# The middle part of a two-layer convolution kernel rebuilt on a ring of 20 tiles, with the depthwise taps taken off TensorE

## The reference, cut to what matters

```
h = gelu(batchnorm(conv1x1(haar(x), w_c1)))        # 8 x 128 x 128 x 128
o = dwconv3x3(h, dw_w, dw_b)                       # nine taps a channel
o = layernorm_chw(o)                               # one mean and variance an image
o = conv1x1(gelu(conv1x1(o, pw1)), pw2)
h2 = o + h
x = x + haar_inverse(gelu(batchnorm(conv1x1(h2, w_c2))))
```

## Time and profile before

| | us |
|---|---|
| median of 3 runs (lowest to highest) | 5953.61 (5949.91 to 5953.89) |
| the profiled execution, its own time | 5952.43 |
| its span, first to last instruction | 5950.4 |
| busy in the span: PE, DVE, ACT, POOL | 5103.1, 4918.3, 4124.4, 220.3 |
| middle part, first y1 load to first load of the third part | 2934.3 to 4505.9 |

### The profile page before, as it was taken

The page is one execution under the profiler, slowest core; times in us unless marked ns, Lnnn a source line. Parts: engine busy times, 40 slices in busy tenths (PEclk is TensorE's granted clock), DMA queues, the critical chain, the costliest instruction groups (busy, mean ns, idle before and its releaser), DMA issues.

```text
span 5950.4 us, 66856 instructions
## 1 busy us (share of the span) xinstructions
PE 5103.1 (86%) x13460; PEld 2331.3 (39%) x13460; DVE 4918.3 (83%) x5569; ACT 4124.4 (69%) x6080; POOL 220.3 (4%) x267
## 2 busy tenths in 40 slices
PE   1889999999999999999868988889887777777775
PEld 0334444444444444444334544445443222222222
DVE  6998988989898898875388888888856888888887
ACT  4877777777777777665245555556546888888887
POOL 0000000000000000000000000000000111111111
PEclk6999999999999999999989999999999999999998
DMA  8999999999999999887612322223216999999999
GB/s 338 370 360 426 427 426 427 420 427 420 427 418 427 427 418 427 341 334 294 251 62 86 110 85 85 85 85 110 87 65 161 237 235 236 236 235 237 235 237 225
DMA packets 279307, 1627.01 MB, mean 273 GB/s; under 512 B 32816, under 2 KB 33200, under 8 KB 115376
## 3 DMA queue, kind: packets, MB, share of 16 engines
q1 hardware_dynamic: 187056, 1022.13, 43.5%
q0 software_dynamic: 36864, 268.45, 21.7%
q10 hardware_dynamic: 55296, 335.57, 13.5%
HBM read 954.94 MB, written 671.09 MB: 273 GB/s over the span
## 4 chain that ended last, share of the span: by engine, by line
PE 55%; DMA 21%; DVE 11%; issue 7%; ACT 4%; DVEq 0%; ACTq 0%; POOLq 0%; SPq 0%; POOL 0%
DMA out_x<-arena 18%; PE ps L678 13%; PE ps L666 11%; PE ps L661 11%; PE ps L785 6%; PE ps L774 4%; PE ps L753 4%; PE ps L744 4%; DMA arena<-in_x 3%; ACT arena L623 2%; DVE arena L1065 2%; DVE arena L1051 2%; PE ps L762 1%; DVE arena L1079 1%; DVE arena L1195 1%
## 5 line engine op out<-in xcount | busy, mean ns | idle before, releaser
L858 PE MATMUL ps<-arena,c2T 128*128 128x512 f32 x2048 | 1033.2, 657 | 380.9 <-ACT arena L616 369.8
L661 PE MATMUL ps<-arena,w_right 128*128 128x512 f32 x2048 | 974.2, 598 | 42.7 <-DVE w_right L1000 22.8
L666 PE MATMUL ps<-arena,w_center 128*128 128x512 f32 x2048 | 967.2, 595 | 24.4 <-DVE arena L1079 24.4
L678 PE MATMUL ps<-arena,w_c1b 128*128 128x512 f32 x2048 | 964.7, 615 | 7.8 <-DVE small L1029 7.6
L1195 DVE SCALAR_TENSOR_TENSOR arena<-arena,taps (+1 forms) x1280 | 860.0, 745 | 4.0 <-issue 0.2
L410 ACT ACTIVATE arena<-ps,small 128x1024 f32<-128x1024 f32 x512 | 568.1, 1110 | 371.1 <-PE ps L666 371.0
L1051 DVE SCALAR_TENSOR_TENSOR arena<-arena,shift 128x2048 f32<-128x2048 f32 x256 | 601.3, 2349 | 250.8 <-PE ps L666 132.5
L858 PEld LDWEIGHTS ps<-arena,c2T 128*128 128x128 f32 x2048 | 405.7, 207 | 1007.7 <-ACT arena L616 565.8
L616 ACT ACTIVATE arena<-ps,small 128x512 f32<-128x512 f32 x1024 | 713.7, 778 | 105.1 <-DVE arena L1294 94.4
L388 ACT ACTIVATE ps<-arena 128x1024 f32<-128x1024 f32 x512 | 526.3, 1028 | 170.2 <-ACT arena L410 160.3
L661 PEld LDWEIGHTS ps<-arena,w_right 128*128 128x128 f32 x2048 | 385.3, 190 | 552.3 <-issue 470.3
(11 more groups left out here) (161 smaller groups left out, 4839.8 us busy)
## 6 DMA issues: line engine op xcount, KB each, us to landing
arena<-in_x SPq DMA_DIRECT2D x400, 1024.0 KB, 15.6
out_x<-arena ACTq DMA_DIRECT2D x256, 1024.0 KB, 8.9
arena<-out_x SPq DMA_DIRECT2D x256, 1024.0 KB, 16.3
out_x<-arena POOLq DMA_DIRECT2D x256, 1024.0 KB, 17.0
arena<-in_x SPq DMA_DIRECT2D x112, 1152.0 KB, 15.4
y_dram<-arena ACTq DMA_DIRECT2D x128, 512.0 KB, 8.5
arena<-y_dram SPq DMA_DIRECT2D x128, 512.0 KB, 3.5
h_dram<-arena SPq DMA_DIRECT2D x256, 256.0 KB, 2.0
```

The costliest lines, as they stand in the source:

```text
L661: mm(ps[:, r, :], w_right[:, :], u_buf[k][:, 2 * r:2 * r + 2, 2:W + 2], start=False, stop=False, skip_group_check=True)
L666: last = mm(ps[:, r, :], w_center[:, :], v_buf[k][:, r * BANK:(r + 1) * BANK], start=False, stop=True, skip_group_check=True)
L678: last = mm(ps[:, 4 + s % 2, :], w_c1b[:, q, :], cells[:, q // 2, q % 2, :, :], start=(q == 0), stop=(q == 3))
L858: last = mm(ps[:, 4 * k + q, :], c2T[:, q, :], h2_in[s // 2][:, k * HC:(k + 1) * HC], start=True, stop=True)
```

## The change: a ring of tiles in place of two planes

The planes `h_pad` and `o_all` go. `h_rows` holds the h of 20 tiles and a row on either side, `o_ring` the o of 20 tiles. One loop without rounds runs on every engine over steps s = 0 to 148, written out, without loop instructions: step s makes h of tile s, finishes o of tile s - 2, and does the old half of tile q = s - 19. The layernorm of an image is done inside of the steps 2 after its last tile (`norm_step`).

Taps: ACT puts the centre tap of a tile (1024 elements) into two PSUM banks, DVE adds five taps there, one instruction of 1024 each, the next tile's taps between those of this one, and `finish_o` adds the sum that POOL has made of the three others and writes o. POOL runs three TENSOR_SCALAR and two TENSOR_TENSOR of 1024 a tile. PE has no taps. `first_conv` and `second_conv` write the same two banks, one after the other. h2 is written over o in the ring by one instruction and stored by one DMA of 512 KB. The Gram matrix is added up in PSUM over an image. The setup tensors of the other parts lie in the arena at other addresses.

```
+POOL_TAPS = [(1, 0), (1, 2), (0, 0)]
+DVE_TAPS = [(0, 1), (0, 2), (2, 0), (2, 1), (2, 2)]
+EARLY = 3
+RING = 20
+OLD_LAG = RING - 1
+        z_bank = ps[:, 0:2, :]
+        def tap_order(s):
+            late = [(s - 2, i) for i in range(EARLY, len(DVE_TAPS) + 1)]
+            early = [(s - 1, i) for i in range(EARLY)]
+            return [(t, i) for pair in zip(late, early) for t, i in pair if 0 <= t < TILES]
...
 SP
-            planes(0, old=False)
-            with sp.Fori(1, B) as b:
-                planes(b)
-            planes(B, new=False)
+            for s in range(TILES + OLD_LAG):
+                q = s - OLD_LAG
+                if s < TILES:
+                    if s >= 2:
+                        sp.wait_ge(h_ready, nth(s - 2))
+                    sp.dma_start(y1_in[s % 2], y1_dram[s]).then_inc(y1_loaded[s % 2], 16)
+                if q >= 0:
+                    sp.wait_ge(h2_ready, nth(q))
+                    if q >= 4:
+                        sp.wait_ge(h2_stored[q % 4], 16 * (q // 4))
+                    sp.dma_start(h2_dram[q], o_ring[q % RING]).then_inc(h2_stored[q % 4], 16)
...
 POOL
+            for t in range(TILES):
+                n = t * POOL_OPS
+                pool.wait_ge(h_ready, nth(t))
...
+                pool_tap(pool_b, t, POOL_TAPS[1])
...
+                pool_tap(pool_a, t, POOL_TAPS[0])
+                if t:
+                    pool.wait_ge(dw_acc, o_made(t - 1))
+                pool.wait_ge(pool_step, n + 2)
+                pool.tensor_tensor(pool_sum, pool_a, pool_b, ALU.add).then_inc(pool_step, 1)
+                pool.wait_ge(pool_step, n + 3)
+                pool_tap(pool_a, t, POOL_TAPS[2])
+                pool.wait_ge(pool_step, n + 4)
+                pool.tensor_tensor(pool_sum[:, first:last], pool_sum[:, first:last], pool_a[:, first:last],
+                                   ALU.add).then_inc(pool_step, 1)
...
 ACT
+            for s in range(TILES + OLD_LAG + 1):
+                q = s - OLD_LAG
+                if s < TILES:
+                    make_h(s)                 # waits: h2_ready of tile s - 20, y1_loaded of s
+                if 0 <= q < TILES:
+                    make_a(q)                 # 128 x 1024 gelu of z_bank; waits: pw1_done of q
+                if q >= 1:
+                    copy_hT(q - 1, 0)
+                b = norm_step(s)
+                if b is not None:
+                    square_root(b + (2 * B + 2))
+                    warm_gelu(b + 1)
+                if s < TILES:
+                    put_tap(s)                # waits: o of tile s - 2 made
+                if q >= 1:
+                    copy_hT(q - 1, 1)
+                if 0 <= s - 2 < TILES:
+                    square_o(s - 2)
...
 PE
+            for s in range(TILES + OLD_LAG + 2):
...
+                if 0 <= q < TILES:
+                    first_conv(q)             # waits: h2_ready of q - 1
...
+                if 1 <= q <= TILES:
+                    turn_h2(q - 1, 0)
+                if q >= 2 and b is None and after is None:
+                    gram_half(q - 2, 1)
+                if 0 <= q < TILES:
+                    second_conv(q)            # waits: a_ready of q
...
+                if 1 <= q <= TILES:
+                    turn_h2(q - 1, 1)
+                    gram_half(q - 1, 0)
...
 DVE
+            for s in range(TILES + OLD_LAG + 2):
...
+                if b is not None:
+                    o_moments(b)
+                for n, (t, i) in enumerate(tap_order(s)):
+                    if i == len(DVE_TAPS):
+                        finish_o(t)           # waits: POOL's sum of t
+                    else:
+                        add_tap(t, i)
...
+                if 0 <= q < TILES:
+                    make_h2(q)                # waits: pw2_done of q
+                if b is not None:
+                    o_weights(b)
```

More of the change, by code:

```diff
@@ L301, in _ @@
             sp.wait_ge(bn1_ready, 1)
[L303 to L318, removed]
[L320 to L327 removed]
+            for s in range(TILES + OLD_LAG):
[9 more added lines that the diff above has]
+                    sp.dma_start(h2_dram[q], o_ring[q % RING]).then_inc(h2_stored[q % 4], 16)
+            for k in range(4):
+                sp.wait_ge(h2_stored[k], 4 * TILES)
             sp.wait_ge(bn2_ready, 1)
@@ L514, in _ @@
             act.wait_ge(bn1_ready, 1)
[L516 to L574, removed]
+            def make_h(t):
+                p = t % RING
+                if t >= RING:
+                    act.wait_ge(h2_ready, nth(t - RING))
+                act.wait_ge(y1_loaded[t % 2], 16 * (t // 2) + 16)
+                y1 = rows(y1_in[t % 2])
+                if p == 0 and t % NT:
+                    nc.scalar.activation(h_rows[:, RING * TROWS + 1, 1:HW + 1], y1[:, 0, :], ACT.Gelu,
+                                         bias=h_bias, scale=h_scale)
+                if p == RING - 1 and t % NT != NT - 1:
+                    nc.scalar.activation(h_rows[:, 0, 1:HW + 1], y1[:, TROWS - 1, :], ACT.Gelu,
+                                         bias=h_bias, scale=h_scale)
+                nc.scalar.activation(h_tile(t), y1, ACT.Gelu, bias=h_bias, scale=h_scale).then_inc(h_ready, 1)
@@ L766, in gram_tile @@
-            def gram_tile(b, j):
-                n = b * (2 * NT) + j * 2
-                pe.wait_ge(gram_added, nth(b * NT + j, 1))
-                for half in range(2):
-                    pe.wait_ge(hT_ready, nth(n + half))
-                    for c in range(4):
-                        last = mm(ps[:, 0, 0:P + 1], hT_buf[half][:, c, 0:P], hT_buf[half][:, c, :],
-                                  start=(half == 0 and c == 0), stop=(half == 1 and c == 3))
-                last.then_inc(gram_done, 1)
@@ L778, in dw_half @@
-            def dw_half(b, j, half, last_tile=False):
-                below = any(dy == 2 for dy, _ in PE_TAPS) and not last_tile
-                pe.wait_ge(h_ready, nth(b * NT + j, -int(below)))
-                pe.wait_ge(dw_put, nth(b * (2 * NT) + j * 2 + half))
-                for n, (dy, dx) in enumerate(PE_TAPS):
-                    last = mm(ps[:, 6 + half, :], tap_diag[:, n, :],
-                              h_pad[:, bass.ds(j * TROWS + (4 * half + dy), 4), dx:dx + HW],
-                              start=False, stop=(n == len(PE_TAPS) - 1), skip_group_check=True)
-                last.then_inc(dw_done, 1)
@@ L790, in planes_step @@
-            def planes_step(b, j, new, old):
-                early = isinstance(j, int)
-                before = old and not (early and j == 0)
-                if old:
-                    first_conv(b - 1, j, back=1 if early and j == 0 else 2)
-                if before:
-                    turn_h2(b - 1, j - 1)
-                if new and not early:
-                    dw_half(b, j - DW_LAG, 0)
-                if before:
-                    gram_tile(b - 1, j - 1)
-                if new and not early:
-                    dw_half(b, j - DW_LAG, 1)
-                if old:
-                    second_conv(b - 1, j)
@@ L828, in _, with first_conv @@
-            pe.wait_ge(bn1_ready, 1)
-            planes(0, old=False)
-            with pe.Fori(1, B) as b:
-                planes(b)
-            planes(B, new=False)
+            def first_conv(q):
+                if q % NT == 0:
+                    pe.wait_ge(w_ready, q // NT + 1)
+                if q:
+                    pe.wait_ge(h2_ready, nth(q - 1))
+                for half in range(2):
+                    last = mm(z_bank[:, half, :], w_pw1b[:, :], o_ring[q % RING][:, half * BANK:(half + 1) * BANK],
+                              start=True, stop=True)
+                last.then_inc(pw1_done, 1)
@@ new lines, in second_conv, with turn_h2 @@
+            def second_conv(q):
+                pe.wait_ge(a_ready, nth(q))
+                for half in range(2):
+                    last = mm(z_bank[:, half, :], pw2T[:, :], a_buf[:, half * BANK:(half + 1) * BANK],
+                              start=True, stop=True)
+                last.then_inc(pw2_done, 1)
+            def turn_h2(q, half):
+                n = q * 2 + half
+                pe.wait_ge(h2_ready, nth(q))
+                if n:
+                    pe.wait_ge(hT_ready, nth(n - 1))
+                for c in range(4):
+                    at_ = half * BANK + c * P
+                    last = nc.tensor.transpose(ps[:, 2, c * P:(c + 1) * P],
+                                               o_ring[q % RING][:, at_:at_ + P], ident[:, :])
+                last.then_inc(hT_done, 1)
@@ new lines, in gram_half @@
+            def gram_half(q, half):
+                b, m = q // NT, q % NT
+                pe.wait_ge(hT_ready, nth(q * 2 + half))
+                if m == 0 and half == 0 and b:
+                    pe.wait_ge(gram_added, b)
+                for c in range(4):
+                    last = mm(ps_gram, hT_buf[half][:, c, 0:P], hT_buf[half][:, c, :],
```

(41 more changed lines are left out.)

336 lines of the change are left out of this document (164 added, 172 removed).

## The result

| | before | after |
|---|---|---|
| median, us (lowest to highest of 5) | 5953.61 (5949.91 to 5954.72) | 5974.98 (5968.61 to 5987.89) |
| span of the profiled execution | 5950.4 | 5969.1 |
| h2 of tile 0 done | - | 3110.1 |
| first load of the third part | 4505.9 | 4523.8 |

The ratio is 1.004, 95% interval 1.0027 to 1.0053: slower, by 21 us and clear of noise, where 88 us faster was forecast. A second comparison on another chip gave 5978.73 against 5951.77, 1.0045 (1.0028 to 1.0061).

A forecast was written before the change was run, and what follows sets the result against it. Before, DVE was full within rounds and all else waited between; after, a loop through SP. h2 of tile 0 at 3096, then 108 x 10.8 + 9, 19 x 6.9 + 3, third part at 4419: 5866 us, range 5740 to 6045.

The forecast's parts named there:

- The loop through SP's order: Beside an old image, y1's load waits behind h2's store; load, gelus, second_conv and make_h2 close a loop of 10.8 us.
- rival B: DVE sets the pace in the middle, 8.5 us a step, needing y1 landed in 2.0 us: 5618 us; chance 0.08.
- PE's clock, 0.2 us a step: second_conv takes some 1.8 us longer at 1.2 GHz; for one in nine that adds 0.2 us a step.
- the 2.25 for full clock: From the start of second_conv to DVE's make_h2, which now needs both halves: 2.25 us.
- D: TensorE stays at 1.2 GHz in second_conv: 1.8 us more a step, 12.4 in all, 6039 us; chance 0.12.
- A: Main forecast: the loop through SP sets a period of 10.8 us (10.0 to 11.5), 5866 us (5780 to 5942); chance 0.68.
- The load, 4.1: y1's load in the loop beside an old image, put at 4.1 us, bounds 3.2 to 4.9.
- The two gelus, 2.30 with the start: On ACT, gelu of h 1.15, gelu of z 1.10, and 0.05 ahead of them: 2.30 us a step.
- Start and end: h2 of tile 0 at 3096; 19 tiles old alone at 6.9 us plus 3; third part's first load at 4419.
- C: POOL sets the pace at 12.7 us a tile, making the kernel slower: 6147 us; chance 0.12.
- DVE's write to PSUM: DVE's taps adding into PSUM cost 0 to 0.1 us more an instruction; the low end was used.
- Layernorm: 30 us between rounds becomes small DVE instructions within steps: 1.5 us each, nine for six images, 3 for the last.

The follow-up runs named there:

- experiment 3: Changed kernel with y1's load issued before the store: 5941.99 us; that with the store held until the load landed: 5820.28; changed kernel storing 8 of 1024 columns: 5863.98.

## Why the prediction was wrong, by its own steps

- *The mechanism was right.* The loop through SP's order was named before any run and is what the rows show; cutting it at SP or at ACT brings the step to 8.3 and 8.6. Without it the forecast would have been rival B's 5618, and the kernel with the load ahead came to 5668.
- *The step that failed is a size: PE's clock, 0.2 us a step.* I let one `second_conv` in nine fall to 1.2 GHz. It took 1.06 us a step: `second_conv` to `make_h2` is 3.08 on average and 2.02 at full clock. By the 1.8 that 1.2 GHz costs, that is six in ten and not one in nine: 25 of 108 lay wholly at 1.2 GHz, 58 in part. This term is 0.86 x 108 = 93 us over its forecast; at its forecast size the time would have been some 5882, an estimate, and so faster than before. Against the 2.45 in the sum only 0.63 a step shows, 68 us, because the 2.25 for full clock was 0.23 too high. I had the two numbers that spoke for more: PE busy for 6.3 of 10.6 with 3 us of pause, and image 0 at 0.77 with gaps of the same kind. Against D I argued that PE would then be busy all the time; it was busy for 807 of 1170. A and D are not rivals: D is a price within A.
- *The load, 4.1.* 4.36 to the landing and 0.12 to the gelu, where 4.1 and 0.05 were forecast: 36 us in all, some 16 of them by the 13 late loads. The bounds 3.2 to 4.9 held it; the reason given, that it queues behind the store, did not (experiment 3).
- *The two gelus, 2.30 with the start.* 0.2 more on average, 16 to 22 us: in one step of each image z waits for the layernorm, and that step takes 13.7 to 15.6. I had put the layernorm on DVE alone.
- *Start and end.* h2 of tile 0 at 3110 for 3096. 4 of these 14 are the first part's addresses, costed at nothing. The larger part is the layernorm of image 0, which stands in no term of the sum: two distances from `finish_o` to `finish_o` are 13.3 and 14.2 (3076.81 to 3104.32) where POOL's pace gives 8.34, 11 us. POOL gave 3 back. The nineteen tiles of the old half alone took 129.7 for 134. In sum 4523.8 for 4419: 14 at the start, 96 in the steps (1270.6 for 1175), less 4.
- *POOL.* 8.3 us a tile for 8.5: 1.118 for the tap (1.1), 2.36 for the add (2.2). C did not come. The estimate of 2.25 for the add from the Trainium skill, GPSIMD Engine Reference, section 3.1, was 0.1 low. The rule of the Trainium skill, SBUF — State Buffer, section "Who interferes with whom", that a DVE instruction with one input in SBUF doesn't hold off POOL, agrees with the trace: all 128 of POOL's first adds took 2.34 to 2.37 us, though DVE was busy for the whole of some and for a tenth of others.
- *DVE's write to PSUM* cost nothing: a tap of 1024 elements takes 1.28 us, as forecast.
- *Layernorm.* 9 us were forecast beside old images and nothing for the first; it cost the 16 to 22 us of z's wait and 11 for the first. With the load ahead the twelve steps of six layernorms hold (8.96 - 8.30) x 108 = 71 us, 12 an image.
- *The range and chances.* Three of A's terms were too low (clock 0.86, load 0.33, z's wait 0.2) and three too high (`second_conv` at full clock 0.23, the issue 0.13, gelu of z to `second_conv` 0.05): the sum, 11.76, is over A's own end of 11.5. The stated range still holds the time, because D was taken into it. I gave slower 0.27; with a loop of 10.8 against 9.8 and a break-even near 11.6, three unknown terms within 0.8 us of the sign called for more.

## What to carry to other kernels

Where an engine or queue runs in program order, follow one item from step to step through the orders of all engines, DMAs included: a load behind a store's wait, used in the same step, puts its whole landing into the step. Starting the load one step earlier took it out of the loop, which was worth 311 us here for three lines; with the taps off PE but the loop closed, the kernel was 21 us slower than before. Whoever moves work to an idle engine must check that its wait doesn't close such a loop anew. PE's part of a loop that holds a pause needs a price at both clocks, 2.02 and 3.82 here, and the low one for more than a few steps: six in ten here. And the granted clock is to be read in the stretch that matters: 0.85 over all was 0.64 in `second_conv`.

## What was not expected of the hardware

A load of 512 KB landed 0.7 to 0.9 us later beside a store of 512 KB, whichever was issued first, while the store landed after 2.9 us when issued first and after 5.1 when issued second. 13 of 108 loads beside the stores took over 5 us. The same first part ran 6 us longer at other SBUF addresses. And PE's clock rose from 0.85 to 0.96 when its pause went, with the same matmuls.
